# Last attention of a two-layer decoder: the residual in a load buffer of its own, and epsilon added on GpSimd

## The reference, cut to what matters

```python
x = x + xattn(layernorm(x), ctx)        # 16 heads of 32, bias bo on the output
x = x + (fp8(layernorm(x)) @ fp8(W).T + bias)
# layernorm(x) = (x - mean) / sqrt(var + 1e-5)
```

## Time and profile before

| | |
|---|---|
| median of 3 runs | 3515.82 us (3511.73 to 3518.59) |
| the profiled execution, its time / its span | 3515.65 us / 3513.9 us |
| busy share of the span: TensorE, weight loads, VectorE, ScalarE, GpSimd | 88%, 66%, 60%, 40%, 37% |
| mean granted TensorE clock, as a share of full speed | 0.950 |
| the last phase, in the profile | from about 2890 us to the end, 16 entries |
| its usual round | 35.35 us |

### The profile page before, as it was taken

One profiled execution on the slowest core, in us unless ns is written; L12 is line 12 of the kernel. 1 busy time (PEld: TensorE's weight loads), 2 busy tenths in 40 slices (PEclk: granted clock), 3 DMA queues, 4 the chain that ended last, 5 costly groups with the idle time before them and its releaser, 6 DMA issues. The chain is left out here.

```text
span 3513.9 us, 72200 instructions
## 1 busy us (share of the span) xinstructions
PE 3089.8 (88%) x23752; PEld 2314.2 (66%) x23768; DVE 2106.1 (60%) x5257; ACT 1400.9 (40%) x4587; POOL 1315.8 (37%) x1962
## 2 busy tenths in 40 slices
PE   6999999999996999999758777777699987988897
PEld 5888888888884777877534333333377765666664
DVE  6666666666764788788552111111266666888885
ACT  4444444444443555555331111111111116676664
POOL 2544544544541444444210000000022225777776
PEclk9999999999997999999869988888899998999998
DMA  3001001001002111111359999999711213222221
GB/s 129 19 18 36 18 18 36 18 18 36 18 19 91 45 63 48 57 62 48 126 235 419 426 425 425 425 425 425 299 60 67 70 51 108 76 73 72 77 70 40
DMA packets 151161, 456.14 MB, mean 130 GB/s; under 512 B 13332, under 2 KB 65816, under 8 KB 130616
## 3 DMA queue, kind: packets, MB, share of 16 engines
q1 hardware_dynamic: 130104, 434.33, 32.0%
q10 hardware_dynamic: 20992, 20.98, 1.7%
HBM read 399.69 MB, written 55.57 MB: 130 GB/s over the span
## 5 line engine op out<-in xcount | busy, mean ns | idle before, releaser
L413 POOL TENSOR_TENSOR cross_prob<-cross_prob,cross_rsum 128x128 f32<-128x128 f32 (+1 forms) x512 | 256.0, 530 | 349.3 <-DVE cross_rsum L797 349.1
L413 POOL TENSOR_TENSOR self_prob<-self_prob,self_rsum 128x128 f32<-128x128 f32 (+1 forms) x512 | 285.6, 584 | 246.1 <-DVE self_rsum L797 246.0
L1796 POOL TENSOR_TENSOR last_prob<-last_prob,last_rsum 128x256 f32<-128x256 f32 x512 | 299.1, 616 | 85.0 <-DVE last_rsum L2131 82.9
L654 ACT ACTIVATE self_prob<-self_S,self_neg_max 128x128 f32<-128x128 f32 (+1 forms) x512 | 212.0, 425 | 199.5 <-DVE self_neg_max L789 199.4
L1225 PE MATMUL experts_H<-moe_w,experts_tok 128*32 128x512 f32 x1024 | 172.5, 836 | 127.8 <-DMA moe_b<-in_L_ffn_w 116.2
L407 POOL TENSOR_TENSOR self_QK_T<-self_QK_T,self_turned 128x512 f32<-128x512 f32 x128 | 164.6, 1286 | 293.8 <-DVE self_QK_T L752 292.0
L1448 POOL MEMSET norm_minus_half<- 128x2 f32 x1 | 0.1, 100 | 692.7 <-POOLq L53 692.7
L2006 ACT ACTIVATE last_prob<-last_S,last_neg_max 128x256 f32<-128x256 f32 x512 | 237.7, 485 | 46.8 <-DVE last_neg_max L2127 44.8
L654 ACT ACTIVATE cross_prob<-cross_S,cross_neg_max 128x128 f32<-128x128 f32 (+1 forms) x512 | 210.2, 429 | 76.0 <-DVE cross_neg_max L789 75.1
L1342 DVE COPY experts_hidT<-experts_T 128x512 f32<-128x512 f32 x32 | 22.1, 692 | 341.0 <-PE experts_T L1236 341.0
L1937 PE MATMUL last_T<-last_ident,last_prob 128*128 128x128 f32 x1024 | 165.5, 285 | 54.6 <-DVE last_probT L2136 31.1
(11 more groups left out here) (313 smaller groups left out, 9795.2 us busy)
## 6 DMA issues: line engine op xcount, KB each, us to landing
moe_w<-in_L_ffn_w SPq DMA_DIRECT2D x64, 4096.0 KB, 36.5
self_x_t<-in_x SPq DMA_DIRECT2D x16, 512.0 KB, 3.6
self_res<-in_x SPq DMA_DIRECT2D x16, 512.0 KB, 3.6
x<-self_res SPq DMA_DIRECT2D x16, 512.0 KB, 2.8
cross_x_t<-x SPq DMA_DIRECT2D x16, 512.0 KB
cross_c_t<-in_ctx SPq DMA_DIRECT2D x16, 512.0 KB, 6.3
cross_res<-x SPq DMA_DIRECT2D x16, 512.0 KB, 3.6
x<-cross_res SPq DMA_DIRECT2D x16, 512.0 KB, 2.8
```

The source lines that it names most:

```text
L413: ins = pool.tensor_tensor(pr, pr, rsum[:, h, t:t + 1].to_broadcast([P, KQ[t]]), ALU.mult)
L654: ins = act.activation(prob[:, h % NP, SOFF[t]:SOFF[t] + KQ[t]], SC[h % G][:, SOFF[t]:SOFF[t] + KQ[t]], ACT.Exp, bias=neg_max[:, h, t:t + ...
L1796: ins = pool.tensor_tensor(pr, pr, rsum[:, h, t:t + 1].to_broadcast([P, S]), ALU.mult)
```

## The change

The residual is loaded into a new tile `res_ld` of its own. SyncE issues that load behind the value load at the step PV2 of the round before, once GpSimd's bias adds of the current entry have read the tile (`res_b`). GpSimd's `res` step reads `res_ld` and writes `res`, and takes over the wait for O1- of the entry before. Both epsilon adds leave VectorE and become GpSimd instructions ahead of the power, each with a semaphore of its own between the two.

```diff
+    RES_GROUP = 2
-    NL, NF = 7, 9
+    NL, NF = 6, 8
+        res_ld = ph.sb("res_ld", [P, T, D])
+        eps = ph.sb("eps", [P, T])
 # SyncE, body(r)
-                    with_res = not isinstance(r, int) and key == RES_STEP
                     if key[0] == "S":
                         sp.wait_ge(s_full, n * H + G * key[1] + G)
-                        if with_res:
-                            res_taken(r - 1)
                         load_keys(following, key[1])
                     elif key[0] == "PV":
                         sp.wait_ge(pv_ok, n * H + G * key[1] + G)
-                        if with_res:
-                            res_taken(r - 1)
+                        if key[1] == RES_GROUP:
+                            sp.wait_ge(res_b, n * T + T)
                         load_values(following, key[1])
+                        if key[1] == RES_GROUP:
+                            sp.dma_start(res_ld[:, :, :], rows(x_in[following])).then_inc(res_in, 16)
...
-                    elif key == ("O", 1) and isinstance(n, int):
-                        res_taken(n)
-                        sp.dma_start(res[:, :, :], rows(x_in[following])).then_inc(res_in, 16)
-                    if with_res:
-                        sp.dma_start(res[:, :, :], rows(x_in[r])).then_inc(res_in, 16)
 # GpSimd
             def rstds(n):
-                pool.wait_ge(ln, NL * n + 5)
+                pool.wait_ge(ln, NL * n + 4)
+                pool.tensor_tensor(rstd[:, 0, :], mv[:, 0, :, 1], eps[:, :], ALU.add).then_inc(with_eps, 1)
+                pool.wait_ge(with_eps, n + 1)
                 pool.tensor_tensor(rstd[:, 0, :], rstd[:, 0, :], minus_half[:, :], ALU.pow).then_inc(ln_pow, 1)
+            pool.memset(eps[:, :], EPS).then_inc(pool_const, 1)
             def res_bias(n):
                 pool.wait_ge(res_in, n * 16 + 16)
+                if not (isinstance(n, int) and n == 0):
+                    pool.wait_ge(a_free[BANK["O", 1]], freed[BANK["O", 1]].at(("O", 1), n - 1) + 1)
                 for t in range(T):
-                    pool.tensor_tensor(res[:, t, :], res[:, t, :], bo_r[:, :], ALU.add).then_inc(res_b, 1)
+                    pool.tensor_tensor(res[:, t, :], res_ld[:, t, :], bo_r[:, :], ALU.add).then_inc(res_b, 1)
             def linear_rstds(n):
-                pool.wait_ge(fl, NF * n + 5)
+                pool.wait_ge(fl, NF * n + 4)
+                pool.tensor_tensor(rstd[:, 1, :], mv[:, 1, :, 1], eps[:, :], ALU.add).then_inc(with_eps_l, 1)
+                pool.wait_ge(with_eps_l, n + 1)
                 pool.tensor_tensor(rstd[:, 1, :], rstd[:, 1, :], minus_half[:, :], ALU.pow).then_inc(fl_pow, 1)
 # VectorE, norm_stats and linear_stats
-                dve.wait_ge(ln, NL * n + 4)
-                dve.tensor_scalar(rstd[:, 0, :], mv[:, 0, :, 1], EPS, None, ALU.add).then_inc(ln, 1)
-                dve.wait_ge(fl, NF * n + 4)
-                dve.tensor_scalar(rstd[:, 1, :], mv[:, 1, :, 1], EPS, None, ALU.add).then_inc(fl, 1)
```

More of the change, by code:

```diff
@@ L1699, in last_phase @@
         (ident_in, b_in, r_in, w8_in, w_hi, w_lo, x_ok, res_in, res_b, stored, ln, ln_pow, a_full, x_hi, scaled, s_full,
-         max_ok, exp_ok, rsum_ok, norm_ok, t_full, pt_dve, pt_act, pv_ok, pool_const, z_hi, z_ok, fl, fl_pow, biased,
+         max_ok, exp_ok, rsum_ok, norm_ok, t_full, pt_dve, pt_act, pv_ok, pool_const, with_eps, with_eps_l, z_hi, z_ok, fl, fl_pow, biased,
          fin) = (
@@ L1703, in last_phase @@
                 "ident_in b_in r_in w8_in w_hi w_lo x_ok res_in res_b stored ln ln_pow a_full x_hi scaled s_full "
-                "max_ok exp_ok rsum_ok norm_ok t_full pt_dve pt_act pv_ok pool_const z_hi z_ok fl fl_pow biased "
+                "max_ok exp_ok rsum_ok norm_ok t_full pt_dve pt_act pv_ok pool_const with_eps with_eps_l z_hi z_ok fl fl_pow biased "
                 "fin").split())
@@ L1734, in _ @@
             sp.dma_start(ident_b[:, :], consts["ident_b"]).then_inc(w8_in, 16)
-            sp.dma_start(res[:, :, :], rows(x_in[0])).then_inc(res_in, 16)
+            sp.dma_start(res_ld[:, :, :], rows(x_in[0])).then_inc(res_in, 16)
             def has_next(n):
@@ L1741, in _ @@
             steps = [(key, off) for key, off, _ in PE_ORDER]
-            RES_STEP = [key for key, off in steps[steps.index((("O", 1), -1)):] if key[0] in ("S", "PV") and off == 0][0]
-            def res_taken(n):
-                sp.wait_ge(a_free[BANK["O", 1]], freed[BANK["O", 1]].at(("O", 1), n) + 1)
             def body(r):
@@ L1787, in _ @@
             pool.memset(minus_half[:, :], -0.5).then_inc(pool_const, 1)
-            pool.wait_ge(pool_const, 1)
+            pool.memset(eps[:, :], EPS).then_inc(pool_const, 1)
+            pool.wait_ge(pool_const, 2)
             rstds(0)
@@ L1800, in res_bias @@
                 pool.wait_ge(res_in, n * 16 + 16)
+                if not (isinstance(n, int) and n == 0):
+                    pool.wait_ge(a_free[BANK["O", 1]], freed[BANK["O", 1]].at(("O", 1), n - 1) + 1)
                 for t in range(T):
-                    pool.tensor_tensor(res[:, t, :], res[:, t, :], bo_r[:, :], ALU.add).then_inc(res_b, 1)
+                    pool.tensor_tensor(res[:, t, :], res_ld[:, t, :], bo_r[:, :], ALU.add).then_inc(res_b, 1)
             def linear_rstds(n):
-                pool.wait_ge(fl, NF * n + 5)
+                pool.wait_ge(fl, NF * n + 4)
+                pool.tensor_tensor(rstd[:, 1, :], mv[:, 1, :, 1], eps[:, :], ALU.add).then_inc(with_eps_l, 1)
+                pool.wait_ge(with_eps_l, n + 1)
                 pool.tensor_tensor(rstd[:, 1, :], rstd[:, 1, :], minus_half[:, :], ALU.pow).then_inc(fl_pow, 1)
             def linear_bias(n):
-                pool.wait_ge(fl, NF * n + 7)
+                pool.wait_ge(fl, NF * n + 6)
                 for t in range(T):
@@ L2109, in linear_quantise @@
                     dve.tensor_scalar(x8[:, t, :], y[:, t, :], mv[:, 1, t, 0:1], rstd[:, 1, t:t + 1], ALU.subtract, ALU.mult, saturate=False).then_inc(fl, 1)
-                dve.wait_ge(fl, NF * n + 7)
+                dve.wait_ge(fl, NF * n + 6)
                 dve.memset(wait_slot[:, 3:4], 0.0)
```

## The result

The changed kernel takes 3496.23 us (median of 5 runs, 3491.88 to 3500.89), the kernel before 3517.48 in the runs beside it (5 runs); the ratio is 0.9942, with a 95% interval of 0.9932 to 0.9953. The medians are 21.3 us apart, and the ratio makes it 20.4; 24.4 were forecast (3491), in a range of 3475 to 3506.

A forecast was written before the change was run, and what follows sets the result against it. TensorE was taken as near full, with 3.7 us idle in a 35.35 us round; 18.0 + 0.2 + 20.8 - 15.6 + 1.0 gave 24.4 us off 3515.65, so 3491 us, range 3475 to 3506.

The forecast's parts named there:

- three stalls: TensorE idles 1.51 us before T1, 1.62 us before T10 and about 0.5 us at T9; the change leaves the last.
- Part 1: Epsilon add L2069 off VectorE: T1 starts without its wait, 1.5 us a round, 18.0 us in twelve rounds plus 0.2.
- part 3: Residual loaded early: GpSimd's adds start at 3255.7 instead of 3259.87, T10's 1.6 us wait goes, 20.8 us in 13 rounds.
- the sum: 18.0 + 0.2 + 20.8 - 15.6 + 1.0 (last two rounds), together 24.4 us off; usual round near 33.45 us.
- Part 2: Epsilon adds of 128x2 on GpSimd: 0.2 us each plus 0.08 handover to the power; the next entry's is hidden.
- Rival E: The new GpSimd add is itself held up; at 3.08 us the kernel is 12 us slower, 3528; 5%.
- The freed place: VectorE's fapply- loses its undisturbed window during GpSimd's DMA wait; F0- starts late, 1.2 us a round, 15.6 us back.
- the alternation: At fapply-, VectorE and GpSimd instructions take turns; the last cast ends at 3260.2 against 3259.04, 1.15 us later.
- B: No collision at fapply- if instructions are luckily spaced: 40.0 us off, 3475.6; 12%.
- C: Full block: L2109 at fapply- waits for GpSimd's whole run, cast 2.3 us late; 10.1 us off, 3505.5; 13%.
- D: GpSimd becomes the bound between the cast's end and the next T1; part 1's gain is gone, 6.4 us off, 3509; 9%.
- there is nothing to win or lose by it there: Said of the granted clock in the last phase: 1.00, the 2.4 GHz level, so no gain or loss.

## Why the prediction was right, and what it missed

**What bounds the phase.** Right: TensorE's order, with three stalls. Each that went shortened the round.

**Part 1, L2069.** Right in the kernel as changed: T1 has no wait. Too strong was the sentence that this form can't run while GpSimd works through back to back: with the residual half alone it slipped in between two of GpSimd's instructions in 8 of 13 rounds and was over in 0.56 or 0.75 us. And its 18.0 us were written down for moving epsilon, while the residual half alone takes most of that stall away too. Its cost hung on where GpSimd's dense run stood, and part 3 moved that. In the sum this made no error, since each stall was counted once. As a statement about which edit earned what it was wrong.

**Part 2, the add's cost.** 0.2 us taken, 0.19 measured, and 0.08 to the power. Rival E had nothing to it.

**Part 3, the residual.** The adds began right behind the power (3213.35), T10's wait went, and nobody waited for the moved load.

**The freed place.** The step argued from two rounds at the end was right, and nearly in its size: 1.15 us from the alternation, and F0- waits 1.17. Cases B and C are refuted, and so is D: no T from T11 on waited in a usual round. That the meeting with GpSimd is the cause is shown by the kernel with the adds behind norm11, where the four instructions take 1.94 us again.

**The sum.** The total came near by luck. A usual round with the clock up takes 33.15 us, against 33.45 forecast, and the usual round before was 35.50 on average, not the 35.35 of the one round that was read. That is 2.35 us a round and 30.6 in 13, where the terms of the sum make 23.4. In the two rounds shown, TensorE's idle time went from 3.72 to 1.77 us, near the 1.9 forecast, and its busy time from 31.63 to 31.35: no line of the prediction has these 0.3 us, and no run isolates them. The step that failed is one sentence at the start: "there is nothing to win or lose by it there", said of the clock. A granted clock of 1.00 in the one round that was read was taken for a fact of the phase, though the same trace has a stretch at 0.50 at 3407 us, and though the prediction itself put a new idle time of 1.2 us just ahead of T9's, with only 0.6 us of transposes between. The loss is 9 rounds of 1.4 us, some 12.4 us in the profiled execution; the kernel with work in the gap gets 14.3 back over the whole run. That the forecast gain was still only 3 to 4 us off is owed to errors on the other side: the 7.2 us more in the rounds, and the last two rounds, which gave 4.8 us in this execution where 1.0 was put down, and 0.4 in the second trace.

**What stays open.** Why the clock falls in 9 of 13 rounds and not in the other 4, though TensorE's idle time looks the same in both (busy 1.72 and 1.73 us in 3.40); why it fell once in the kernel before behind 1.97 us at T10, and in no usual round with the epsilon half alone, where that wait was up to 1.93; and why an instruction of VectorE sometimes gets in between two of GpSimd's and sometimes waits for the end of the whole run.

## What to carry to other kernels

When a stall goes, look at what its engine was doing for others by standing still: here GpSimd's wait for a DMA was the window in which VectorE's instructions ran undisturbed. Place GpSimd's long runs away from those VectorE instructions that they hold up, or cut them into pieces that fit into waits which are there anyway; this gave more than the whole change. And count a new idle time of TensorE twice, once for itself and once for the clock behind it. Here that second price fell due in 5 or 9 of 13 rounds where a wait of 1.1 to 1.2 us lay 0.6 us ahead of one of 0.5, in none where three lay 5 to 6 us apart, and in 0 to 3 of 13 where a long wait (1.3 to 2.0 us) lay 1.7 us behind a short one. These are counts from a few traces, and no run separates the distance of two waits from their length.

## What the hardware showed that was not expected

Two idle times of TensorE of 1.17 and 0.50 us, with 0.6 us of transposes between them, were followed in 9 of 13 rounds by some 3.4 us at 1.2 GHz, at 1.4 us a round, in both traces of the changed kernel. The kernel before had more idle time in a round, 1.5 us at T1, and 0.5 and 1.3 to 2.0 at T9 and T10 with 1.7 us of work (T9 and PV1) between, and fell in one round of 13; with the two-tensor add in 3 of 13. Four useless products that filled 0.9 us of the wait made the whole kernel 14.3 us faster.

An add of two elements per lane on VectorE took 0.17 us, 0.56, 0.75, 1.55, 1.9 or 3.08 us, according to where it met GpSimd's run; with two tensors it took 0.16, 1.5 or 3.06. GpSimd paid less: its norm10 took 1.55 us and not 1.18.
